# First attention's last three heads: exponentials and values split into high and low halves, their product as three single-pass products

## The reference

```python
q, k, v = (split_heads(q), split_heads(k), split_heads(v))      # b=2, HEADS=4, DIM_HEAD=64
qn = rmsnorm(q, qn_g) * SCALE
kn = rmsnorm(k, kn_g)
attn = jnp.einsum('bhid,bhjd->bhij', qn, kn)                    # 1024 x 1101 for each of 8 heads
attn = jnp.where(full_mask[:, None, None, :], attn, -jnp.finfo(attn.dtype).max)
attn = jax.nn.softmax(attn, axis=-1)
out = jnp.einsum('bhij,bhjd->bhid', attn, v)
return out @ Wo.T + bo
```

## Time and profile before

| | |
|---|---|
| median of 3 runs | 820.66 us (820.35 to 820.71) |
| the profiled execution, its time / its span | 824.63 us / 822.5 us |
| busy in it | PE 760.1, PEld 621.8, DVE 529.4, ACT 399.3, POOL 322.2 us |
| granted TensorE clock, mean | 0.974 |
| costliest group | L650, x288, 147.8 us, mean 595 ns |

### The profile page before, as it was taken

The page is one execution under the profiler, slowest core; times in us unless marked ns, Lnnn a source line. Parts: engine busy times, 40 slices in busy tenths (PEclk is TensorE's granted clock), DMA queues, the critical chain, the costliest instruction groups (busy, mean ns, idle before and its releaser), DMA issues.

```text
span 822.5 us, 12847 instructions
## 1 busy us (share of the span) xinstructions
PE 760.1 (92%) x4881; PEld 621.8 (76%) x4881; DVE 529.4 (64%) x1163; ACT 399.3 (49%) x699; POOL 322.2 (39%) x281
## 2 busy tenths in 40 slices
PE   7889989999999999999999989984699999999996
PEld 7755545657755564679889888883689999999995
DVE  7767875774568683357455498885747756667552
ACT  3655644573466344563472245433035765557650
POOL 6502001200201022066361043334326878888794
PEclk9999999999999999999999999995699999999998
DMA  7000000000000100100030201121202444544522
GB/s 186 2 0 1 1 0 1 1 0 1 1 1 1 51 4 0 52 1 3 1 98 1 103 2 53 52 77 39 103 27 84 128 124 148 136 109 117 135 33 33
DMA packets 21509, 39.31 MB, mean 48 GB/s; under 512 B 4913, under 2 KB 16905, under 8 KB 19145
## 3 DMA queue, kind: packets, MB, share of 16 engines
q1 hardware_dynamic: 14793, 30.07, 11.2%
q0 software_dynamic: 6656, 8.43, 5.9%
HBM read 29.96 MB, written 8.40 MB: 47 GB/s over the span
## 4 chain that ended last, share of the span: by engine, by line
PE 57%; DVE 14%; ACT 4%; issue 3%; POOL 3%; DVEq 0%; ACTq 0%
PE ps L481 17%; PE ps L650 8%; PE ps L1173 6%; PE ps L1176 5%; PE ps L754 5%; PE ps L475 2%; PE ps L671 2%; PE ps L672 2%; PE ps L612 2%; DVE sm L1616 1%; DVE rep L1810 1%; PE ps L1096 1%; DVE Pb L1620 1%; DVE sm L1625 1%; POOL out_dram L2732 1%
## 5 line engine op out<-in xcount | busy, mean ns | idle before, releaser
L650 PE MATMUL ps<-PT,VA 128*65 128x512 f32 (+1 forms) x288 | 147.8, 595 | 3.3 <-ACT PT L2119 3.1
L2119 ACT ACTIVATE PT<-ps 128x512 f32<-128x512 f32 x128 | 76.1, 595 | 70.5 <-PE ps L672 70.1
L481 PE MATMUL ps<-GT,wh 128*128 128x258 f32 (+1 forms) x768 | 94.7, 284 | 0.4 <-DVE GT L1908 0.4
L481 PEld LDWEIGHTS ps<-GT,wh 128*128 128x128 f32 x768 | 92.7, 189 | 0.6 <-DVE GT L1908 0.6
L2732 POOL DMA_INDIRECT out_dram<-ye,idx x40 | 69.7, 1743 | 19.7 <-issue 10.9
L2416 ACT ACTIVATE het<-ps,b1e 128x514 f32<-128x514 f32 x64 | 44.3, 692 | 58.3 <-PE ps L481 54.0
L1943 DVE TENSOR_TENSOR he<-het,he 128x514 fp32r<-128x514 f32 x64 | 46.4, 726 | 35.6 <-ACT he L1972 35.1
L671 PE MATMUL ps<-QA,KA 128*128 128x512 f32 x144 | 67.9, 472 | 0.8 <-ACT QB L1972 0.8
L2466 POOL TENSOR_TENSOR rs<-rs,half 128x4 f32<-128x4 f32 (+2 forms) x19 | 18.1, 955 | 121.2 <-DVE rs L1214 93.3
L612 PE MATMUL ps<-KA,QA 128*128 128x368 f32 x192 | 60.0, 418 | 3.1 <-ACT mrt L1972 0.8
L2610 POOL DMA_INDIRECT gt<-y_dram,idx x40 | 46.3, 1158 | 41.7 <-DVE gate L1898 32.0
(11 more groups left out here) (291 smaller groups left out, 1664.9 us busy)
## 6 DMA issues: line engine op xcount, KB each, us to landing
wr<-in_w1e_dram SPq DMA_DIRECT2D x8, 1024.0 KB, 5.0
wr<-in_w2e_dram SPq DMA_DIRECT2D x8, 1024.0 KB, 4.8
x<-in_x_dram SPq DMA_DIRECT2D x4, 512.0 KB, 6.5
w<-in_w_dram SPq DMA_DIRECT2D x2, 1024.0 KB, 4.8
y_dram<-yr SPq DMA_DIRECT2D x3, 512.0 KB, 3.0
out_dram<-x SPq DMA_DIRECT2D x3, 512.0 KB, 4.0
b2r<-in_b2r_dram SPq DMA_DIRECT2D x8, 128.0 KB, 3.3
gt<-y_dram,idx POOLq DMA_INDIRECT x40, 3.3
```

Of the source, the lines that this page charges most:

```text
L481: op = pe.matmul(o, l, r, start=n == 0, stop=n == len(calls) - 1)
L650: pe.matmul(bank[6 + hf][0:65, :], VA[b][0:K, kt, h, :], PT[u % 4][0:K, :], start=kt == 0, stop=kt == 8).then_inc(p_pv, 1)
L2119: a.activation(PT[u % 4][0:K, :], bank[4 + u % 2][0:K, :], ACT.Exp, bias=0.0 if K == 128 else mcol[:, b:b + 1]).then_inc(a_exp, 1)
```

## The change

In heads 5, 6 and 7 (`SPLIT`) the exponentials and the values are split too. ScalarE takes the exponential twice from the same bank: once into the f32r tile `PH` (three buffers), once in fp32 into `PT`. The low half is PT - PH, written over PT as `PL` (f32r), by GpSimd in heads 5 and 6 (`exponentials_low`) and by DVE in head 7. The values' high halves `VH` are made by ScalarE in head 4 (`values_high`, three copies), their low halves `VL` by GpSimd. TensorE multiplies `VL`*`PH` and `VH`*`PH` where the fp32 product stood (`pv_high(u-1)`), and `VH`*`PL` two steps later (`pv_low(u-3)`; the last three of a head fall in the next head's first three steps). So a bank is complete three units later: `ot` moves from u = 9 and 0 to u = 12 and 3, and in between side work that would use the occupied bank 6 or 7 all goes to bank 3 (`side_bank`). A PSUM bank of scores is free once the second exponential has been taken (`a_raw`), and `PH` is reused once the low half of three units before is made.

```diff
+SPLIT = (5, 6, 7)
...
+def split_at(hi, u):
+
+    return 18 * (hi - SPLIT[0]) + u
...
+def side_bank(hi, u, n):
+    if n % 2 == 0:
+        return 3
+    if (hi - 1 in SPLIT and u < 5) or (hi in SPLIT and 9 <= u < 13):
+        return 3
+    return 7 if u < 9 else 6
...
+                    pe.wait_ge(a_exp, 18 * hi + u + 1)
+                    for n, V in enumerate((VL, VH)):
+                        pe.matmul(bank[6 + hf][0:65, :], V[0:K, kt, h, :], PH[split_at(hi, u) % 3][0:K, :],
+                                  start=kt == 0 and n == 0, stop=False)
...
+                    if hi < 7:
+                        pe.wait_ge(g_wlo, 7 + split_at(hi, u) + 1)
+                    else:
+                        pe.wait_ge(v_init, 2 + u + 1)
+                    pe.matmul(bank[6 + hf][0:65, :], VH[0:K, kt, HEADS[hi][1], :], PL[split_at(hi, u) % 4][0:K, :], start=False,
+                              stop=kt == 8).then_inc(p_pv, 1)
...
-                    busy[m] = (a_exp, 18 * hi + u + 1)
-                    if u:
-                        pv(u - 1)
+                    if hi in SPLIT:
+                        busy[m] = (a_raw, 8 + split_at(hi, u) + 1)
+                        if u:
+                            pv_high(u - 1)
+                        if u >= 3:
+                            pv_low(hi, u - 3)
+                        elif hi > SPLIT[0]:
+                            pv_low(hi - 1, u + 15)
...
+                if hi == 7:
+                    for u in range(15, 18):
+                        pv_low(hi, u)
...
                 for u in range(18):
-                    made["unit"] = u
-                    if u == 9:
+                    made["unit"], made["head"] = u, hi
+                    if hi == 7:
+                        K = 128 if u % 9 < 8 else SC
+                        v.wait_ge(a_raw, 8 + split_at(hi, u) + 1)
+                        v.tensor_tensor(PL[split_at(hi, u) % 4][0:K, :], PT[split_at(hi, u) % 4][0:K, :], f(PH[split_at(hi, u) % 3][0:K, :]),
+                                        ALU.subtract).then_inc(v_init, 1)
+                    if u == (12 if hi in SPLIT else 9):
                         ot(hi, 0)
...
+                        if 3 <= k < 39:
+                            a.wait_ge(g_wlo, 7 + k - 2)
+                        elif k >= 39:
+                            a.wait_ge(v_init, 2 + k - 38)
+                        a.activation(PH[k % 3][0:K, :], bank[4 + u % 2][0:K, :], ACT.Exp, bias=bias_).then_inc(a_exp, 1)
                         a.wait_ge(p_pv, n - 3)
-                    a.activation(PT[u % 4][0:K, :], bank[4 + u % 2][0:K, :], ACT.Exp,
-                                 bias=0.0 if K == 128 else mcol[:, b:b + 1]).then_inc(a_exp, 1)
+                        a.activation(PT[k % 4][0:K, :], bank[4 + u % 2][0:K, :], ACT.Exp, bias=bias_).then_inc(a_raw, 1)
...
+            def exponentials_low(hi):
+                for u in range(18):
+                    K = 128 if u % 9 < 8 else SC
+                    g_.wait_ge(a_raw, 8 + split_at(hi, u) + 1)
+                    g_.tensor_tensor(PL[split_at(hi, u) % 4][0:K, :], PT[split_at(hi, u) % 4][0:K, :], f(PH[split_at(hi, u) % 3][0:K, :]),
+                                     ALU.subtract).then_inc(g_wlo, 1)
+                    yield
...
+            drain(exponentials_low(5))
...
             g_.memset(f(lrow[:, :, :]), 0.0).then_inc(g_zero, 1)
-            lnf(0)
-            lnf(1)
+            ln_ = spaced(lnf_beside(0), lnf_beside(1))
+            merge(exponentials_low(6), (ln_, SIDE_RATE[6]))
+            drain(ln_)
             w1_lora(0)
```

## The result

After: 834.5 us, median of four runs (833.06 to 837.15), against 820.68 us for four runs of the kernel before: 1.016 times as long [1.014, 1.018]. Slower as forecast, but by 13.8 us and not by 2.4, and outside the range. The profiled execution took 837.15 us, its span 835.4.

The account below looks back on a forecast made before the run. TensorE was taken to bound heads 5 to 7. Terms -3.4 (head 5), -0.2 (head 6), +5.5 and -2.1 (head 7), +0.6, +0.3 and +1.7 (clock) gave +2.4 us on 820.66: 823.1 us, range 819.0 to 827.5.

Parts of the forecast that it names:

- head 7's ring: Head 7's first steps: ScalarE's copy and exponentials, DVE's low half and tsp wait in a loop; unit 4's product 5.5 us later.
- GpSimd's power in head 6: Head 6: the first power ends 9.8 us in, behind low halves and memset; before, 7.6 us in.
- the low half's 1.29 us: Heads 5 and 6: each low-half subtraction on GpSimd takes 1.29 us.
- the product's pace of 0.23 us: TensorE, heads 5 to 7: f32r products follow at 0.23 us from start to start; a unit gains 0.164 us.
- From its end to the transposes took 288.70 - 285.95 = 2.75 us, which stays: Head 6: the transposes follow the power's end by 2.75 us as before, so they start at 12.6 us, not 10.4.
- -0.2: Head 6: ends at 34.3 us against 34.5, so -0.2 us; bounds -2.9 and +9.
- GpSimd and DVE in each other's way: Rival, head 6: low halves on GpSimd take 1795 ns each, +9 us, total 832; chance 0.12.
- The clock: Heads 6 and 7: half-clock stretch after TensorE idles, +1.7 us, bounds 0 and 3.4.
- from there to `ffn1`: Head 7 after unit 4's product: TensorE bound again, 13 units give -2.1 us; the bare last unit adds +0.6.
- Head 5: Head 5: 18 fp32 products go, 51 f32r ones come, -3.65 us; with ScalarE's loss, -3.4 us.
- My 0.25 us for ScalarE: Head 5: ScalarE, with 18 more exponentials, runs just behind in the first nine units, costing 0.25 us.
- The bounds, -3.65 and 0: Head 5: limits given around the forecast of -3.4 us.

Follow-up runs that it names:

- x2: Kernel before plus 18 subtractions on GpSimd in head 6 whose results nobody reads: 827.2 us, ratio 1.005.
- x6: Changed kernel with memset in head 5, GpSimd waiting after head 6's powers for normalised rows, row additions moved to head 7: 827.9 us, ratio 1.008.
- r1: The changed kernel run once more, nothing altered: 833.7 us, ratio 1.015 to the kernel before.
- x1: Changed kernel without the 54 low-half subtractions; ScalarE's second exponential writes the low product's tile: 819.4 us, ratio 0.997.
- x5: x1 with ScalarE's second exponential left out too, all three f32r products reading one tile: 816.9 us, ratio 0.995.
- x10: x9 with head 7's two GpSimd row additions cut in eight, each waiting for one more DVE low half: 815.8 us, ratio 0.993.
- x4: Changed kernel with DVE's low half in head 7 put behind the next step's w1_lora side step: 828.8 us, ratio 1.008.
- x8: x1 with DVE's first-half ot in heads 5 to 7 at u = 13 instead of 12: 817.5 us, ratio 0.995.
- x9: x6 with the edits of x4, x8's ot move, and head 6's second-half ot at u = 4 in head 7: 820.2 us, ratio 0.998.
- x11: Changed kernel with each GpSimd low half in head 6 waiting for the end of the one before: 835.3 us, ratio 1.015.

## Why the prediction was wrong

Right: the direction, head 7's ring to 0.4 us in every step (head 7: +4.3 us forecast and perhaps a clock stretch of 1.7, +6.2 measured), GpSimd's power in head 6 (9.67 us in, forecast 9.8), the low half's 1.29 us (mean of 36) and the product's pace of 0.23 us.

The step that failed is head 6's "From its end to the transposes took 288.70 - 285.95 = 2.75 us, which stays". It took 4.67 and 5.26, since GpSimd's subtractions hold DVE's `TENSOR_SCALAR`, and behind these stood a maximum and an update that TensorE waited for. Without the clock head 6 was 39.03 us: +4.55 instead of -0.2. x2 gives 5.4 us for this alone (with one half-clock stretch of 3.4 us in it), and x6 takes most of it back. Even without the ports the 2.75 us would not quite have stayed: in x6 it was 3.3 and 3.6, and the first 0.6 of that is `ot`, which the change itself had moved ahead of the normalisation.

My rival *GpSimd and DVE in each other's way* had the right pair of engines and the wrong loser. It priced GpSimd's low halves at 1.8 us when held by DVE; GpSimd kept 1.29 and DVE was held. That its 832 us lies near the measured 834.5 is luck. I had read the lock from the maxima of subtractions, looked for collisions of the same kind only, and never asked which other DVE instructions of head 6 work from SBUF to SBUF.

The clock was mis-sized: +1.7, with 3.4 as its bound. Its measured part in head 6 was 4.06 us in the profile and 1.56 in r1. In head 7 it counts behind the ring, where TensorE is the bound. The product of unit 4 came 5.9 us later than before, where I forecast 5.5; from there to `ffn1` it took 20.2 us, before 20.0, where I forecast 1.5 less. The 3.41 us at half clock behind the ring can account for up to 1.7 of that difference; how much it is, no run shows. That head 6's two stretches come from the waits I hadn't forecast is likely and not shown: no profile without these waits has half clock there (x1, x5 to x10), but x4 has the waits and no half clock.

Head 5 gave 1.7 us and not 3.4. My 0.25 us for ScalarE was 0.7 (x5), and `ot` on the step of a `max_tile`, which I costed at nothing, was 0.7 (x8); about 0.6 stays open. The bounds, -3.65 and 0, held it.

Sum by the same terms, profile against profile: head 5 -1.7, head 6 +4.55 and its clock +4.06, head 7 +6.2 with its clock: +13.1; the span grew by 12.9.

## What to carry to other kernels

Before moving work to GpSimd, list DVE's `tensor_scalar` from SBUF to SBUF in the stretch, and its instructions with two inputs in SBUF (x9), and look which of them another engine waits for: each can wait for a whole GpSimd instruction or more, and the wait shows as duration, not as idle time. GpSimd need not do less; it has to be silent at the right moment, by a wait for DVE's result (x6, x10). An instruction with one input in SBUF need not be on the list: the moments kept 0.41 us. In an order written by hand, a step that gets a wait must stand behind whatever closes a loop over other engines (x4, x9).

## What the runs showed of the hardware

- One DVE instruction can be held over more than one GpSimd instruction: `rs`, ready at 282.81, let subtractions that began at 282.82 and 284.07 pass and ended at 285.38. With a gap of 0.14 us between subtractions it got in at once (x11).
- Moments with one input in SBUF (`BATCH_NORM_STATS2`) took 0.41 us beside subtractions (x2), as in the kernel before, while two-input subtractions on DVE of 0.68 us took 2.29 and 2.90 against row additions of 128x1024 (x9).
- A pair of normalisations takes 0.73 us alone and 2.66 beside two subtractions of 2.57 together: the waits are nearly the whole of it, and little of its own time comes on top.
- The same instructions of head 6 took 39.0, 40.6 and 43.1 us, with 0, 3.4 and 13.7 us of them at half clock and the same distances from power to transposes.
